# A two-layer mixture-of-experts kernel on one core: waits and small steps put in other places of four engines' orders, and the first layer's stores cut in two

## The chip, the core and the metric

The kernel runs on one core of a Trainium2 chip. Its time is the device time of one execution in microseconds (us). TensorE is called PE, VectorE DVE, ScalarE ACT, GpSimd POOL and SyncE SP; SP issues most of the transfers. PEld is PE's row of weight loads, and a small q behind an engine's name means its sequencer, which also does register loads.

## What is computed

The input x is 64 batches of 64 tokens by 1024 numbers. Each layer adds a correction to x:

```python
x = x + L0_ffn(L0_cond(x, id0))        # adapter: 64x64 matrix of the batch, over the tokens
x = x + L1_ffn(L1_cond(x, id1))        # adapter: 1024x1024 matrix of the batch
# L0_ffn: logits = y @ router_w.T + b; top 2 of 8 experts; h = y @ A_e (rank 16); out = sum gate*h @ B_e * 0.5
# L1_ffn: y @ base_w.T + b  +  0.5 * sum over the top 2 of 16 experts of gate * (y @ A) @ B_e (rank 64)
```

All of it is float32. The second layer's large products are made of three passes of split numbers (hi times hi, hi times lo, lo times hi), where `hi` is a rounded copy made by ACT and `lo` is the rest, made by DVE.

## The kernel before

Each engine has an order of its own, written out by hand; semaphores tie them together. There are three stages.

**First layer** (`two_groups(n)` on PE, n = 0 to 7, `NS` = 8). The batches go in 16 groups of four (`NG`), two to a round n. For a group PE makes z = x times router and A weights (`z_of`, L1573), mixes the tokens (`y_of`), DVE works out the gates of both groups of the next round (`gates0`, a chain of some 17 small operations from L1113 on, then four of L1117 that write `hw0`), PE turns `hw0` (`turn_h0`, L1619), and PE multiplies with the experts' B (`expand`, four quarters q). DVE adds x to each quarter (`add_x`, L1135) into one of two buffers `x1g`; `expand(g)` may write quarter q only when `add_x` has taken quarter q of group g-1. SP stores a group's `x1g` (1 MB, `store_x`, L457) when its four adds are done, then loads x for six groups later (`load_x`). `add_x(g, 0)` waits until the store of group g-2, from the same buffer, has landed. The first rounds of DVE's loop also hold constants for the second layer (`second_layer_constants`, L1066 to L1075) and register loads from `table`, the plan of the second layer (`w_used` L398, `start_of` L401, `alone` L406). PE does two of these loads after its last `expand`, behind eight filler products (`keep_going(8)`, L1626).

**Adapters of the second layer** (loops over u, the adapters in use, and j, the pairs of batches of an adapter; `step` on ACT and DVE, `y_of_pair` on PE). PE multiplies a pair with its adapter, turns the pair before it (`turn`, after chunk 1 of 8) and multiplies the turned pair with A and the router (`rh_of`, L1686, near the end). In the step at an adapter's last pair (`u_next` is given) ACT and DVE also split the next adapter's eight weight chunks (`w_chunks`, `low_chunks`, L830 and L1141), and `y_turned` (ACT L798, DVE L1217) splits the turned y between them. A pair with one batch (`lone`) takes PE two passes instead of three.

**Base product, routing and experts.** For 32 tiles t of 128 tokens PE runs `base_part(t, n)`, n = 0 to 15, three products each; ACT and DVE split the tile in quarters (`y_high` L877, `y_low` L1276). `expert_high` and `expert_low` (L896, L1286) split the 16 experts' B. DVE chooses the experts, gives each token its row, and makes one-hot tables `hot_a` (`tile_of_rows`) and `hot_b` (`row_of_rows(n)`, L1365, eight, two buffers). PE multiplies these (`row_sums(n)`, L1785, eight), which gives `rows`, the list by which POOL gathers tokens for the experts (L707); PE turns the gathered rows (`turn_hw`, L1795). After tile 7 the experts' products run between the base parts, then the rest of the tiles with the sum into the output.

## Time and profile before

| | |
|---|---|
| three runs, us | 1110.53, 1114.62, 1116.79 (median 1114.62) |
| profiled execution, us | 1110.44, its span 1108.8 |
| busy in the span, us | PE 1075.5, PEld 916.6, DVE 673.4, ACT 501.5, POOL 219.8 |
| granted clock of PE, mean | 0.995 of full |
| chain that ended last | PE 77%, DMA 7%, DVE 7%, ACT 3%, SPq 3%, issue 2% |

The span is the time from the first to the last record of the profiled execution. A busy PE holds waits between matmuls too short to show; what a change of order can give back is PE's idle time and what its clock loses after it. The chain names, from the end backwards, what each piece of work was released by.

### The profile page before, as it was taken

Reading aid. Unit: us, or ns where it says so; the run is one execution under the profiler, and the core shown is the slowest. Engines: PE = TensorE matmul, PEld = TensorE weight load, DVE = VectorE, ACT = ScalarE, POOL = GpSimd, SP = SyncE. Lnnn points to the kernel's source line nnn. Section 1 sums busy time; section 2 is a strip of 40 time slices with the busy share of each in tenths; the row PEclk is TensorE's granted clock in tenths of the full one; section 3 lists DMA queues with packets and bytes.
Section 4 is the critical chain, followed back from the end, with each engine's and each line's share of the span. In section 5 each row is a group of like instructions: output and inputs, shape, how many; then the busy total and the mean of one; then the engine's idle time right before and its main releaser. Section 6 shows DMA issues by size and latency. Waiting matters only on the chain.

```text
span 1108.8 us, 21632 instructions
## 1 busy us (share of the span) xinstructions
PE 1075.5 (97%) x5844; PEld 916.6 (83%) x5845; DVE 673.4 (61%) x1231; ACT 501.5 (45%) x1021; POOL 219.8 (20%) x354
## 2 busy tenths in 40 slices
PE   7989999999999999999999999999999999999998
PEld 7989878888887888888888877877777888888887
DVE  5778843755738457564546588545555466666666
ACT  1122123745638456564536642145555434443444
POOL 2211010110202011110101000155553322222220
PEclk9999999999999999999999999999999999999999
DMA  9678683673947648583677342279999999999996
GB/s 304 242 280 330 221 327 96 236 268 126 340 158 246 231 160 311 196 271 124 229 236 233 96 133 85 78 285 346 356 345 353 344 396 357 335 356 323 333 337 205
DMA packets 126125, 283.57 MB, mean 256 GB/s; under 512 B 28146, under 2 KB 35570, under 8 KB 124146
## 3 DMA queue, kind: packets, MB, share of 16 engines
q1 hardware_dynamic: 96592, 180.59, 46.1%
q0 software_dynamic: 29216, 102.25, 26.4%
q8 instruction: 29, 0.48, 0.2%
q14 instruction: 30, 0.25, 0.1%
q10 hardware_dynamic: 258, 0.01, 0.0%
HBM read 181.50 MB, written 101.29 MB: 255 GB/s over the span
## 4 chain that ended last, share of the span: by engine, by line
PE 77%; DMA 7%; DVE 7%; ACT 3%; SPq 3%; issue 2%; DVEq 0%; ACTq 0%
PE psum L1562 17%; PE psum L1564 16%; PE psum L1563 16%; PE psum L1686 4%; PE psum L1573 4%; DMA xp<-act_scratch 3%; PE psum L1809 3%; PE psum L1810 3%; PE psum L1678 3%; PE psum L1704 2%; PE psum L1706 2%; PE psum L1687 2%; PE psum L1818 1%; SPq L548 1%; ACT w L896 1%
## 5 line engine op out<-in xcount | busy, mean ns | idle before, releaser
L1562 PE MATMUL psum<-base_hi,xp_hi 128*128 128x512 f32 (+3 forms) x520 | 204.3, 393 | 4.4 <-DVE xp_lo L1276 4.2
L1563 PE MATMUL psum<-base_lo,xp_hi 128*128 128x512 f32 (+3 forms) x520 | 198.9, 383 | 0.0
L1564 PE MATMUL psum<-base_hi,xp_lo 128*128 128x512 f32 (+3 forms) x520 | 198.7, 382 | 0.0
L1562 PE MATMUL psum<-w,xp_hi 128*128 128x512 f32 x448 | 181.2, 404 | 0.0
L1564 PE MATMUL psum<-w,xp_lo 128*128 128x512 f32 x448 | 176.8, 395 | 0.0
L1563 PE MATMUL psum<-w,xp_hi 128*128 128x512 f32 x448 | 176.6, 394 | 0.0
L699 POOL DMA_DIRECT2D raw<-w1T x112 | 59.2, 528 | 414.8 <-DVE w L1141 393.4
L1141 DVE TENSOR_TENSOR w<-raw,w 128x1024 fp32r<-128x1024 f32 x112 | 132.2, 1220 | 11.5 <-ACT w L830 8.5
L877 ACT ACTIVATE xp_hi<-xp 128x256 fp32r<-128x256 f32 x124 | 51.2, 416 | 170.3 <-PE psum L1564 158.1
L1562 PEld LDWEIGHTS psum<-base_hi,xp_hi 128*128 128x128 f32 x520 | 98.1, 189 | 27.7 <-DVE xp_lo L1276 5.4
L1276 DVE TENSOR_TENSOR xp_lo<-xp,xp_hi 128x256 fp32r<-128x256 f32 x124 | 51.7, 424 | 108.5 <-ACT xp_hi L877 107.9
L1564 PEld LDWEIGHTS psum<-base_hi,xp_lo 128*128 128x128 f32 x520 | 98.1, 189 | 18.1
L1563 PEld LDWEIGHTS psum<-base_lo,xp_hi 128*128 128x128 f32 x520 | 98.2, 189 | 15.7
L707 POOL DMA_INDIRECT hwn<-rh_scratch,rows x80 | 75.8, 947 | 173.0 <-DVE rows L1375 112.1
L830 ACT ACTIVATE w<-raw 128x1024 fp32r<-128x1024 f32 x104 | 105.5, 1057 | 5.1 <-PE psum L1564 5.1
L1564 PEld LDWEIGHTS psum<-w,xp_lo 128*128 128x128 f32 x448 | 84.3, 188 | 19.6
L1562 PEld LDWEIGHTS psum<-w,xp_hi 128*128 128x128 f32 x448 | 84.5, 189 | 17.8 <-issue 1.2
L1563 PEld LDWEIGHTS psum<-w,xp_hi 128*128 128x128 f32 x448 | 84.6, 189 | 16.8
L943 ACT ACTIVATE x1t<-x1t,bias 128x128 f32<-128x128 f32 x256 | 78.1, 387 | 19.5 <-DMA x1t<-act_scratch 19.5
L1212 DVE COPY yp<-psum 128x512 f32 x28 | 19.4, 691 | 108.5 <-PE psum L1564 108.5
L790 ACT ACTIVATE yp<-psum 128x512 f32 x28 | 16.8, 599 | 135.6 <-PE psum L1564 135.6
L1198 DVE TENSOR_TENSOR xp_lo<-xp,xp_hi 128x512 fp32r<-128x512 f32 x58 | 39.9, 688 | 52.3 <-ACT xp_hi L780 52.3
(293 smaller groups left out, 1957.8 us busy)
## 6 DMA issues: line engine op xcount, KB each, us to landing
raw<-w1T POOLq DMA_DIRECT2D x120, 512.0 KB, 6.8
delta_scratch<-dl SPq DMA_DIRECT2D x80, 512.0 KB, 4.1
xp<-act_scratch SPq DMA_DIRECT2D x74, 256.0 KB, 3.3
act_scratch<-yT SPq DMA_DIRECT2D x72, 256.0 KB, 2.5
act_scratch<-x1g SPq DMA_DIRECT2D x16, 1024.0 KB, 5.2
x1t<-act_scratch SPq DMA_DIRECT2D x64, 256.0 KB, 4.8
out<-x1t SPq DMA_DIRECT2D x62, 256.0 KB, 5.4
xg<-xT SPq DMA_DIRECT2D x15, 1024.0 KB, 9.2
```

The source lines that it names most:

```text
L699: pool.dma_start(raw[:, i, :], w1T[bass.ds(a, 1), i, :, :].rearrange("a p k -> p (a k)")).then_inc(raw_in[i], 16)
L707: pool.indirect_dma_start(hwn[s % HRING][:, :], None, rhs[0:NB, :, :].rearrange("b c z -> (b c) z"), bass.IndirectOffsetOnAxis(ap=rows[:, ...
L830: act.activation(w_hi[:, i, :], raw[:, i, :], ACT.Copy).then_inc(w_hi_done, 1)
L877: act.activation(xp_hi[:, ks, :].rearrange("p i (b c) -> p b i c", b=2), xp[:, t % 2, :, ks, :], ACT.Copy).then_inc(yh_done, 1)
L943: last = act.activation(x[:, :, i, :], x[:, :, i, :], ACT.Identity, bias=bias[:, i:i + 1])
L1141: tt(w_lo[:, i, :], raw[:, i, :], w_hi[:, i, :].bitcast(F32), ALU.subtract).then_inc(w_lo_done, 1)
L1276: tt(xp_lo[:, ks, :].rearrange("p i (b c) -> p b i c", b=2), xp[:, t % 2, :, ks, :], xp_hi[:, ks, :].bitcast(F32).rearrange("p i (b c) -> ...
L1562: mm(out, a_hi, b_hi, start=start, stop=False, skip_group_check=True)
L1563: mm(out, a_hi, b_lo, start=False, stop=False, skip_group_check=True)
L1564: return mm(out, a_lo, b_hi, start=False, stop=stop, skip_group_check=True)
L1573: last = mm(z_ps[:, m, :], xg[slot][:, i, m * P:(m + 1) * P], p0[:, i, :], start=i == 0, stop=i == KC - 1)
L1686: mm(rh_ps, yq_hi[:, i, :], q2[:, i, :], start=i == 0, stop=False, skip_group_check=True)
```

## The change

Six edits, all of order but one:

1. `store_x` stores a group in two halves of 512 KB, each when its own two adds are done; in memory a half is 1 KB per partition and batch where the whole was 2 KB. The counts on `x1_out` are doubled to match.
2. `second_layer_constants` is cut in two. `sorting_constants` (six operations) stands in round 1 ahead of the adds of group 2, not behind them; `rank_constants` (two) in round 2 ahead of the adds of group 4. DVE's load of `used` follows these, and its loads of `total` and `one` stand in round 3 ahead of the adds of group 6; all three stood in round 2 behind the adds.
3. PE's loads of `used` and `total` stand in round 6 between the filler products and `turn_h0(7)`, not behind the last filler.
4. In a step with new weights, `y_turned` stands behind the first split chunk, not the second, on ACT and DVE.
5. On ACT, `expert_high(6)` and `(7)` stand inside the quarters of tile 2, not ahead of them.
6. `row_sums(n)` stand at n = 5, 7, ..., 15 of tile 6 and n = 1, 3 of tile 7, not at n = 1, 3, ..., 15 of tile 6.

```diff
             def store_x(g):
-                sp.wait_ge(x1_added, 4 * g + 4)
-                sp.dma_start(x1s[g * GB:(g + 1) * GB, :, :].rearrange("b p (i c) -> p b i c", c=C),
-                             x1g[g % 2][:, :, :, :]).then_inc(x1_out[g % 2], 16)
+                for h in range(2):
+                    ks = slice(h * KC // 2, (h + 1) * KC // 2)
+                    sp.wait_ge(x1_added, 4 * g + 2 * h + 2)
+                    sp.dma_start(x1s[g * GB:(g + 1) * GB, :, h * C * KC // 2:(h + 1) * C * KC // 2].rearrange(
+                        "b p (i c) -> p b i c", c=C), x1g[g % 2][:, :, ks, :]).then_inc(x1_out[g % 2], 16)
...
-                w_chunks(range(2))
+                w_chunks(range(1))
                 y_turned(j)
-                w_chunks(range(2, KC // 2))
+                w_chunks(range(1, KC // 2))
...
             keep(0)
-            expert_high(6)
-            expert_high(7)
             for t in range(2, FIRST + 1):
                 for q in range(4):
                     if t == FIRST and q == 3:
                         hw_high(0)
                     y_high(t, q)
+                    if t == 2 and q % 2 == 1:
+                        expert_high(6 + q // 2)
...
-            def second_layer_constants():
+            def sorting_constants():
...
+            def rank_constants():
+                dve.wait_ge(const_split_hi, 3)
                 for first, raw_part in ((0, q1raw), (R1 + E1, margin_raw)):
...
-                    dve.wait_ge(x1_out[g % 2], (g - g % 2) * 8 + 16)
+                    dve.wait_ge(x1_out[g % 2], (g - g % 2) * 16 + 16)
...
+                if n == 1:
+                    sorting_constants()
+                if n == 2:
+                    rank_constants()
+                    dve.wait_ge(table_ready, 1)
+                    used = w_used(dve)
+                if n == 3:
+                    total = start_of(dve, used)
+                    one = alone(dve, 0)
                 if n == NS - 2:
                     gates0(n + 1)
                 add_x(2 * n, 0)
                 add_x(2 * n, 1)
-                if n == 1:
-                    dve.wait_ge(const_split_hi, 3)
-                    second_layer_constants()
-                if n == 2:
-                    dve.wait_ge(table_ready, 1)
-                    used = w_used(dve)
-                    total = start_of(dve, used)
-                    one = alone(dve, 0)
...
                     keep_going(8)
+                    pe.wait_ge(table_ready, 1)
+                    used = w_used(pe)
+                    total = start_of(pe, used)
                     turn_h0(n + 1)
...
-                    if t == FIRST - 2 and n % 2 == 1:
-                        row_sums(n // 2)
+                    if t == FIRST - 2 and n % 2 == 1 and n > 3:
+                        row_sums((n - 5) // 2)
+                    if t == FIRST - 1 and n in (1, 3):
+                        row_sums(6 + n // 2)
```

DVE's order changes in the middle of rounds 1 and 2 of the first layer. Before, from the adds of group 2 (`x1g0<-psum,xg2`) to the gates of round 2 (the first row on `sm`):

```order
L1135 TENSOR_TENSOR x1g0<-psum,xg2 128x2x4x64 x4
L1066 TENSOR_SCALAR desc1<-idx 128x16
L1067 CAST iota<-idx 128x128
L1068 TENSOR_SCALAR tok<-idx 128x32
L1069 TENSOR_SCALAR tok<-tok 128x32
L1071 CAST ones<-raw 128x128
L1072 CAST before<-raw 128x128
L1075 TENSOR_TENSOR q2<-q1raw,q2 128x8x80
L1075 TENSOR_TENSOR q2<-margin_raw,q2 128x8x40
L1113 TENSOR_TENSOR sm<-psum,rbias 128x16 x2
```

The same place with the change (its line numbers are other ones):

```order
L1071 TENSOR_SCALAR tok<-tok 128x32
L1073 CAST ones<-raw 128x128
L1074 CAST before<-raw 128x128
L1140 TENSOR_TENSOR x1g0<-psum,xg2 128x2x4x64 x4
L1118 TENSOR_TENSOR sm<-psum,rbias 128x16 x2
```

Eight operations have left the place between the adds and the gates: six went ahead of the adds, and the two on `q2` a round later.

PE's order changes at the end of the first layer. Before, from the last filler products to the first matmul of the adapters:

```order
L1626 MATMUL psum<-b0_hi 128x512 x8
L398 TENSOR_LOAD table
L398 ISA x2
L401 ISA
L401 TENSOR_LOAD table
L401 ISA x2
L1717 UNCONDITIONAL_BRANCH
L1717 ISA
L427 TENSOR_LOAD table
L427 ISA x2
```

With the change:

```order
L1632 MATMUL psum<-b0_hi 128x512 x8
L1725 UNCONDITIONAL_BRANCH
L1725 ISA
L427 TENSOR_LOAD table
L427 ISA x2
```

Two register loads left this place; they stand behind the filler products of round 6, ahead of the four transposes of `hw0`.

ACT's order changes at the start of the base product. Before, from the copy of tile 0's sums (`nat0`) to that of tile 1's; `w<-raw` are the experts, `xp_hi<-xp` the quarters of tile 2:

```order
L887 ACTIVATE nat0<-psum 128x512
L887 ACTIVATE nat0<-psum 128x472
L896 ACTIVATE w<-raw 64x1024 x4
L877 ACTIVATE xp_hi<-xp 128x2x2x64 x4
L887 ACTIVATE nat1<-psum 128x512
L887 ACTIVATE nat1<-psum 128x472
```

With the change:

```order
L889 ACTIVATE nat0<-psum 128x512
L889 ACTIVATE nat0<-psum 128x472
L879 ACTIVATE xp_hi<-xp 128x2x2x64 x2
L898 ACTIVATE w<-raw 64x1024 x2
L879 ACTIVATE xp_hi<-xp 128x2x2x64 x2
L898 ACTIVATE w<-raw 64x1024 x2
```

The first two quarters of tile 2 moved ahead of all four expert operations, the last two ahead of two of them.

## Rows read from the trace of the kernel before

**Rows 1.** windows: busy us of PE, PEld, DVE, ACT, POOL; clock, DMA

```profile
0.00:145.00 145.00, 131.04 (x1065) 126.27 (x1067) 106.65 (x347) 25.65 (x55) 22.65 (x98) 1.00 0.76 276
```

**Rows 2.** waits of PE: in total, times, longest us

```profile
PE psum L1562 <- DVE xp_lo L1276: 4.2, 6, 1.4
...
PE psum L1562 <- DVE x1g L1135: 0.8, 1, 0.8
```

**Rows 3.** timeline, 50 to 75 us: start, duration, engine, line, idle before

```profile
50.50 0.17 DVE L1066 TENSOR_SCALAR desc<-idx 128x16 f32<-128x16 f32 x1
...
53.18 0.38 DVE L1113 TENSOR_TENSOR sm<-psum,rbias 128x16 f32<-128x16 f32 x2
...
58.12 0.66 PE L1619 MATMUL psum<-ident,hw 128*128 128x128 f32 x4 [1.69 <-DVE hw L1117]
...
63.77 0.69 DVE L1135 TENSOR_TENSOR x1g<-psum,xg 128x512 f32<-128x512 f32 x1 [2.31 <-PE psum L1564]
...
69.95 0.38 DVE L1113 TENSOR_TENSOR sm<-psum,rbias 128x16 f32<-128x16 f32 x2 [2.90 <-issue]
...
74.88 0.66 PE L1619 MATMUL psum<-ident,hw 128*128 128x128 f32 x4 [1.98 <-DVE hw L1117]
```

**Rows 4.** end of the first layer: chain, table loads, timelines of DVE and PE

```profile
135.81 4.24 DMA act_scratch<-x1g
...
L398 PEldq TENSOR_LOAD <-table x1: 502/502/502, 140.1 to 140.1; - x1
...
142.47 0.75 DVE L1193 TENSOR_TENSOR xp_hi<-xp,xp_hi 128x256 fp32r<-128x256 f32 x2
...
144.87 0.47 PE L1704 MATMUL psum<-w,xp_hi 128*128 128x512 f32 x1 [1.68 <-issue]
```

**Rows 5.** timeline and window around 356 us, two adapter changes in a row

```profile
356.15 0.38 PE L1686 MATMUL psum<-q,yq_hi 128*128 128x240 f32 x1 [2.19 <-DVE yq_lo L1217]
...
358.28 0.42 DVE L1193 TENSOR_TENSOR xp_hi<-xp,xp_hi 128x256 fp32r<-128x256 f32 x1
...
359.10 0.77 PE L1704 MATMUL psum<-w,xp_hi 128*128 128x512 f32 x1
...
360.00:362.00 2.00, 2.00 (x6) 1.52 (x5) 2.00 (x3) 2.00 (x3) 0.92 (x2) 0.50 0.95 304
```

**Rows 6.** timelines of ACT and DVE at the first tiles of the base product

```profile
639.91 4.31 ACT L896 ACTIVATE w<-raw 64x1024 fp32r<-64x1024 f32 x4
...
640.08 2.47 DVE L1286 TENSOR_TENSOR w<-raw,w 64x1024 fp32r<-64x1024 f32 x2
```

**Rows 7.** timelines and window, 685 to 725 us: the row sums and after

```profile
687.70 0.42 ACT L877 ACTIVATE xp_hi<-xp 128x256 fp32r<-128x256 f32 x1 [2.26 <-PE psum L1564]
...
690.37 0.42 ACT L877 ACTIVATE xp_hi<-xp 128x256 fp32r<-128x256 f32 x1 [2.25 <-PE psum L1564]
...
693.00 2.35 DVE L1365 TENSOR_TENSOR hot_b<-iota,place_f 128x1024 fp32r<-128x1024 f32 x2
...
694.37 1.31 PE L1785 MATMUL psum<-hot_a,hot_b 128*128 128x80 f32 x8 [2.69 <-DVE hot_b L1365]
...
696.00:698.00 2.00, 2.00 (x6) 1.63 (x5) 0.00 (x0) 0.00 (x0) 0.00 (x0) 0.50 0.05 17
...
698.08 1.15 PE L1785 MATMUL psum<-hot_a,hot_b 128*128 128x80 f32 x8
...
700.47 1.06 PE L1785 MATMUL psum<-hot_a,hot_b 128*128 128x80 f32 x8
...
713.98 1.02 POOL L707 DMA_INDIRECT hwn<-rh_scratch,rows  x1 [112.13 <-DVE rows L1375]
...
722.33 0.38 PE L1795 MATMUL psum<-ident,hwn 128*128 128x128 f32 x2
```

**Rows 8.** DMA issues, 650 to 720 us: queue, count, KB each, us to landing

```profile
base_scratch<-nat SPq DMA_DIRECT2D x5, 492.0 KB, 2.9
...
margin<-side_scratch SPq DMA_DIRECT2D x1, 640.0 KB, 6.6
```

More of the change, by code:

```diff
@@ L473, in _ @@
                 for s in range(2):
-                    sp.wait_ge(x1_out[s], (b // (2 * GB)) * 16 + 32)
+                    sp.wait_ge(x1_out[s], (b // (2 * GB)) * 32 + 48)
                 sp.dma_start(xp[:, bass.ds(slot_of(1, total), 1), h, :, :].rearrange("p a i c -> p (a i) c"),
@@ L477, in _ @@
             for s in range(2):
-                sp.wait_ge(x1_out[s], 16 + 16 * (NG // 2))
+                sp.wait_ge(x1_out[s], 16 + 32 * (NG // 2))
             def load_pair(j):
@@ L689, in _ @@
                 for s in range(2):
-                    pool.wait_ge(x1_out[s], (b // (2 * GB)) * 16 + 32)
+                    pool.wait_ge(x1_out[s], (b // (2 * GB)) * 32 + 48)
                 pool.dma_start(xp[:, bass.ds(slot_of(0, total), 1), h, :, :].rearrange("p a i c -> p (a i) c"),
@@ L693, in _ @@
             for s in range(2):
-                pool.wait_ge(x1_out[s], 16 + 16 * (NG // 2))
+                pool.wait_ge(x1_out[s], 16 + 32 * (NG // 2))
             with pool.Fori(1, used + 1) as u:
@@ L856, in _ @@
             for s in range(2):
-                act.wait_ge(x1_out[s], 16 + 16 * (NG // 2))
+                act.wait_ge(x1_out[s], 16 + 32 * (NG // 2))
             with act.Fori(0, used) as u:
@@ L1240, in low_chunks @@
                             w_low(u_next, i)
-                low_chunks(range(2))
+                low_chunks(range(1))
                 y_turned(j, 0)
@@ L1245, in step @@
                 y_turned(j, 1)
-                low_chunks(range(2, KC // 2))
+                low_chunks(range(1, KC // 2))
                 x_low(j + 1, 0, one)
@@ L1260, in _ @@
             for s in range(2):
-                dve.wait_ge(x1_out[s], 16 + 16 * (NG // 2))
+                dve.wait_ge(x1_out[s], 16 + 32 * (NG // 2))
             with dve.Fori(0, used) as u:
@@ L1644, in two_groups @@
                     z_of(2 * n + 4, 1)
+                return (used, total) if n == NS - 2 else None
             pe.wait_ge(ident_done, 2)
@@ L1665, in _ @@
             for n in range(NS):
-                two_groups(n)
+                counts = two_groups(n)
+                if n == NS - 2:
+                    used, total = counts
             keep_going(8)
-            pe.wait_ge(table_ready, 1)
             def turn(v):
@@ L1714, in _ @@
             pe.wait_ge(const_split, 3)
-            used = w_used(pe)
-            total = start_of(pe, used)
             with pe.Fori(0, used) as u:
```

## The prediction

> **What bounds the kernel now.** I read the table of windows first, to see how much of PE's time is idle, then PE's chain of waits, to see who ends the idle time, and then the timeline at each place that the change touches. PE is the bound: 1075.5 of the 1108.8 us of the span are busy, so the edits can give back at most some 33 us. The first layer holds 14 of them in its 145 us, start-up included, and its DMA share is 0.76, so the transfers have gaps there [rows 1]. In the whole table of PE's waits only a few entries are long, and each lies where an edit works. I take them in order of time. Times of before are quoted throughout, and all of it is one profiled execution.
>
> **The rounds' gates (edit 2).** At 58.12 PE begins to turn `hw0` of round 2 after 1.69 us of idleness, at 74.88 that of round 3 after 1.98 us; both times the gates on DVE are late [rows 3]. What makes them late stands ahead of them on DVE: from 50.50 to 53.18, 2.68 us of constants, and in the next round 2.90 us in which DVE sits idle by "issue" before 69.95, which are its register loads [rows 3]. Both exceed PE's wait, so with them gone PE's data come first and the waits go: 1.69 + 1.98 = 3.67 us. The moved work lands where DVE waits for PE: 2.31 us idle before 63.77 [rows 3]. The two `q2` operations read 960 columns, where the add of 512 took 0.69 us, so 1.3 us, and one load of three is a third of the 2.90, 1.0 us: together they just fill that gap. In round 1 the six others, the 1.4 us that are left of the 2.68, need such a gap too. In round 3 the two other loads (1.9 us) go ahead of the adds of group 6, where DVE is idle less; the adds may start a microsecond late, but the next `expand` asks for them one quarter at a time and over 2 us later. Behind them stand the gates of round 4, which can be late by a few tenths. I take 3.6 us, with 2.5 and 3.7 as ends.
>
> **The end of the first layer (edits 1 and 3).** PE is idle 1.68 us before its first adapter product at 144.87 [rows 4], so its fillers ended at 143.19. Its data are complete at 143.22, when DVE ends the split of pair 0 [rows 4]. The rest is PE's sequencer: it begins the first of three table loads at 140.1 [rows 4] and comes to the product 4.8 us later, 1.6 us a load with what stands between. Without two of them it could be there at 141.7, so that the fillers' end and the split bound it, both 143.2: a gain of 1.65 us. Where the two loads go, in round 6, PE waits for the gates behind its fillers anyway, and the sequencer runs ahead, as 140.1 against fillers that end at 143.19 shows; without that cover they would cost their 3.2 us there.
>
> The cut stores move these two bounds too. A store of 1 MB took 4.24 us to land and released DVE's adds of group 15 [rows 4]; the one before it delayed those of group 14, and through them PE, 0.8 us [rows 2]. A transfer of 492 KB lands in 2.9 us [rows 8]. So the second half lands about 1.3 us sooner after the same add, PE loses its 0.8 us of waiting, its fillers end at 142.4, and the split of pair 0 ends near 141.9. Together the adapters start about 2.5 us sooner. If halves land no sooner it is 1.65; if the sequencer needs its 1.68 us for other things than the loads, only the 0.8.
>
> The price of the cut is in the packets: 512 more of 1 KB per group, 32 on each of 16 DMA engines. No row has a 1 KB packet, so I bound it. Below it is nothing: the bytes are the same. Above: 640 KB in 4096 packets of 160 bytes landed in 6.6 us [rows 8]. The two stores, 1 MB in 4.24 us and 492 KB in 2.9, give 2.6 us for moving 1 MB and 1.6 for the rest. Less that rest it is 5.0 us for 256 packets an engine, 20 ns each with their bytes. 32 of them are 0.6 us a group, against gaps that are 24% of the stage [rows 1]. I take nothing, as the gaps hide it; SP's second issue, 0.4 us a group, is hidden as well, SP being idle between groups.
>
> A rule speaks against this edit. The Trainium skill, "DMA: Bandwidth & Descriptors", section "Measured", says to batch transfers to at least 1 MiB, and its section "Anatomy of one DMA" gives an estimate of 2.0 us plus bytes by 436 GB/s: 4.4 us for the whole store, 3.2 us for a half, two halves 6.4 us if one came after the other. The rows, 4.24 and 2.9 us, agree with the two single figures. By the rule the stores would cost 2 us more a group; but only the last half is waited for, so the sum by its figures would be 1.2 us sooner where rows give 1.3.
>
> **The step with new weights (edit 4).** PE waits for the split of turned y once, 2.19 us at 356.15 [rows 5], where two adapters change in a row and DVE is busy all the time, 2.00 of 2 us [rows 5]. One chunk (1.2 us) fewer stands ahead of it now. But the same chunk then stands ahead of the split of the next pair, which ends where it did, at 358.70 [rows 5], and PE's next product began at 359.10 [rows 5]. DVE's work is the same in sum, so what the edit gives at one wait it takes at the next: 0.4 us. PE's clock fell to 0.50 here [rows 5], for some 7 us; even at 1.00 PE would wait for DVE's copy of y a little later, so at most 0.8 us come back. Lower end: nothing.
>
> **The experts' split on ACT (edit 5).** At 639.91 ACT does four expert operations in 4.31 us before the quarters of tile 2 [rows 6], and PE's longest wait for a low quarter is 1.4 us, at 645.3 [rows 2]. With the first two quarters ahead, these are done at 640.8; then DVE is the limit, busy with experts until 642.55 [rows 6], so its two quarters end at 643.3, before PE's need at 643.9. The wait goes: 1.4 us. The four operations themselves are needed by DVE only 12 us later.
>
> **The row sums (edit 6).** PE wants `hot_b` after two parts of tile 6 and waits 2.69 us, to 694.37 [rows 7]; DVE's first two are 1.2 us each from 693.00 on [rows 7]. Four parts take 2.67 us (687.70 to 690.37 [rows 7]). Asked for four parts later, PE comes at 694.35 by its own work: the wait goes, with nothing to spare. After that wait the clock was 0.50 [rows 7], and the step from the first sums to the second took 3.71 us against 2.39 for the next one [rows 7]: 1.3 us, and 0.2 more in the sums. So 2.69 + 1.5 = 4.2 us; if the wait shrinks only by half and the clock still falls, 1.3.
>
> What is late next: the last sums end about 711.5, 1.6 us sooner than before, while PE is 4.2 us sooner. POOL's first gather then starts at 712.4 instead of 713.98 [rows 7], the second 1.5 us later, and gathers land in 2.6 us, so at 716.5. PE wants them at 722.33 - 4.2 = 718.1 [rows 7]. That leaves 1.6 us. The later gathers stay ahead by more.
>
> **The sum.** 3.6 + 2.5 + 0.4 + 1.4 + 4.2 = 12.1 us. Against the profiled execution's own 1110.44 that is 1098.3; against the median of the three runs, 1114.62, it is 1102.5. I predict 1100.5, between these. The lower ends add to 2.5 + 0.8 + 0 + 1.4 + 1.3 = 6.0, the upper to 3.7 + 2.6 + 0.8 + 1.4 + 4.3 = 12.8. What a measurement of this kernel can tell from no change is about 0.5%, 5.6 us.
>
> **The rivals.**
> - *The row sums or the gathers are still waited for* (0.18). The margin is 0.02 us for `hot_b` and 1.6 for the gathers. For it: DVE's place between its fixed chain and PE is exact only in this execution. Against it: both engines start that stretch from the same tile. It costs about 3 us of the 12.1: 1103.5.
> - *The first layer gives nothing* (0.10). Loads of x are issued behind the stores, and a PE that runs 3.6 us ahead could find them late. For it: most of the stage's idle DMA time lies in a few gaps. Against it: stores, and so loads, move ahead with PE. Then 12.1 - 6.1 = 6.0 remain: 1106.5.
> - *A new half-clock stretch* (0.06). Waits of about 2 us in other places could make the clock fall as at 356.15; each costs the wait and up to 3.5 us at half speed [rows 5]. Two leave about 1.5 us: 1111.
> - *More than I forecast* (0.07): the clock no longer falls at 356, and the runs above 1110 lose what set them apart. 1095.
> - *Slower: packets of 1 KB at half rate* (0.03). If each extra packet cost as much as a whole one of 2 KB, 80 ns by the 2.6 us of moving for 32 packets an engine, the 16 stores would add 41 us to the 0.76 of 145 [rows 1], 151 us in all. With some 12 us at the stage's start and end that no transfer can fill (an estimate) it would last 163 us, 18 more, and with the 6.0 us of the other edits the whole would end near 1122. It decides against the change, by over 0.5%, from about 67 ns a packet on; the bound above is 20.
>
> The forecast itself has 0.56. **How the numbers follow.** 1100.5 is the likeliest case. The range 1094 to 1108 holds the forecast's 1096 to 1104, the rival with the row sums, the one without the first layer and most of the faster one; outside are the half-clock case, the slower one and the tails, under 0.2. Faster by over 0.5% (below 1109): the forecast, the first two rivals and the faster one, less what scatter of the runs takes, 0.87. Within: 0.10. Slower: 0.03.
>
> **What would show it.** PE's waits at L1619 for `hw` near 58 and 73 us gone; the first adapter product near 138.7 (144.87 - 3.6 - 2.5); the wait for y's split shrunk to about 1 us and followed by one for the split of the pair; no wait for the low quarter of tile 2; row sums entered with under 0.3 us of waiting and a clock of 1.00; the first gather about 10 us sooner. I would be wrong if stores of 512 KB took 4 us or more to land, if loads of x held up L1573, or if a clock of 0.50 appeared at a place where it was not.

## The result, and the profile after

The changed kernel took 1101.84 us in the median of four runs (1100.9 to 1102.03), the kernel before 1112.57 beside it (also four, 1110.49 to 1116.79), and 1100.5 was predicted, 1.34 us less. The measurement gives a ratio of 0.9888 with a 95% interval of 0.985 to 0.9926. Its ratios, here and below, are not quotients of the two medians: that would be 0.9904 here, and elsewhere the two differ by up to 0.0014. Its profiled execution took 1100.9 us with a span of 1099.3, 9.5 us less than the span of before.

The sum had worked with 12.1 us, and the two profiles differ by 9.5, so I laid the two traces beside each other at events that both have. First PE's waits in the changed kernel (us in total, times, longest us), the rows that answer to [rows 2]:

```profile
PE psum L1826 <- DVE fin L1482: 3.4, 4, 1.9
PE psum L1714 <- DVE xp_hi L1199: 2.1, 1, 2.1
...
PE psum L1568 <- DVE xp_lo L1204: 1.9, 1, 1.9
PE psum L1568 <- DVE xp_lo L1282: 1.6, 3, 0.6
PE psum L1625 <- DVE hw L1122: 1.2, 2, 1.0
...
PE psum L1696 <- DVE yq_lo L1223: 1.0, 1, 1.0
```

The waits for the low quarters fell from 4.2 us to 1.6, those for the adds and for `hot_b` are gone. New is the second kind of `xp_lo`, 1.9 us at L1204: the split of a pair of batches in the adapters' stage, for which PE did not wait before. The same places in the windows and timelines, as [rows 1], [rows 3], [rows 4], [rows 5] and [rows 7] show them of before (a timeline row is the start, the duration, the engine and line, what it does, and in brackets the idle time ahead of it and what ended that; a row of a window ends in the granted clock, the DMA share and GB/s, and the clock has two levels in these rows, 1.00 and 0.50):

```profile
0.00:145.00 145.00, 138.16 (x1096) 132.38 (x1098) 107.65 (x349) 26.74 (x57) 24.74 (x102) 1.00 0.81 283
...
55.72 0.49 PE L1625 MATMUL psum<-ident,hw 128*128 128x128 f32 x3
...
70.66 0.60 PE L1625 MATMUL psum<-ident,hw 128*128 128x128 f32 x4
...
137.69 0.75 DVE L1199 TENSOR_TENSOR xp_hi<-xp,xp_hi 128x256 fp32r<-128x256 f32 x2
...
138.55 0.47 PE L1714 MATMUL psum<-w,xp_hi 128*128 128x512 f32 x1
...
352.37 0.38 PE L1696 MATMUL psum<-q,yq_hi 128*128 128x240 f32 x1 [1.04 <-DVE yq_lo L1223]
...
356.45 0.77 PE L1714 MATMUL psum<-w,xp_hi 128*128 128x512 f32 x1 [2.07 <-DVE xp_hi L1199]
...
690.74 1.06 PE L1793 MATMUL psum<-hot_a,hot_b 128*128 128x80 f32 x8
693.05 0.98 PE L1793 MATMUL psum<-hot_a,hot_b 128*128 128x80 f32 x8
...
696.00:698.00 2.00, 2.00 (x15) 1.79 (x14) 1.93 (x4) 0.28 (x1) 0.00 (x0) 1.00 0.00 0
...
708.32 1.28 POOL L709 DMA_INDIRECT hwn<-rh_scratch,rows  x1 [108.17 <-DVE rows L1381]
...
714.01 0.38 PE L1803 MATMUL psum<-ident,hwn 128*128 128x128 f32 x2
```

The turns of rounds 2 and 3 have no bracket: no wait. The first adapter product stands at 138.55, where 138.7 was predicted, 6.3 us sooner than before. The row sums enter without a wait at full clock. But `turn_hw` is 8.3 us sooner, not 12. What lies between is shown by the chain of waits (start, duration, what), the timelines of POOL and PE, and a window:

```profile
137.80 3.42 DMA act_scratch<-x1g
141.52 0.46 issue
142.07 0.39 SPq L477
...
143.47 5.17 DMA xp<-act_scratch
148.83 0.64 ACT xp_hi L782
149.67 0.70 DVE xp_lo L1204
```

```profile
142.74 0.53 POOL L701 DMA_DIRECT2D raw<-w1T  x1 [19.04 <-issue]
...
150.77 0.69 PE L1568 MATMUL psum<-w,xp_hi 128*128 128x512 f32 x1 [1.92 <-DVE xp_lo L1204]
...
152.00:154.00 2.00, 2.00 (x6) 1.52 (x6) 2.00 (x6) 0.82 (x3) 0.00 (x0) 0.50 1.02 414
```

The last half store is issued at 137.80 and lands 3.42 us later. SP loads x of pair 1, the adapters' second pair, in two transfers, the first issued at 142.07, the second at 143.47. POOL waits for that landing and begins at 142.74 with eight loads of the next adapter's weights, 4 MB. The second transfer of x takes 5.17 us beside them, PE waits 1.92 us and then runs at a clock of 0.50. In the kernel before POOL's first load stood at 148.43, behind both transfers (146.65 and 148.04), and the second landed in 3.4 us, 0.2 us ahead of ACT's need.

To follow this through all kernels I use distances between events that each has, so that the start, which varies, drops out. "Round 0" is the start of PE's first turn of `hw0`; then come the time from it to the turn of round 7, from there to the first adapter turn, to the second adapter turn, to ACT's first copy of `nat`, to DVE's first `hot_b`, to PE's first `turn_hw`, and to ACT's last `y_high`. They are differences of starts in the timelines of one profile each.

| kernel | round 0 | to round 7 | to 1st turn | to 2nd turn | to `nat` | to `hot_b` | to `turn_hw` | to last `y_high` |
|---|---|---|---|---|---|---|---|---|
| before | 26.73 | 103.99 | 16.09 | 11.03 | 481.00 | 54.16 | 29.33 | 367.33 |
| changed | 26.19 | 100.62 | 13.69 | 14.69 | 481.94 | 52.25 | 24.63 | 366.13 |
| e1 edit 2 only | 30.33 | 100.64 | 16.12 | 11.05 | 481.46 | 54.16 | 29.32 | 367.69 |
| e2 edit 1 only | 26.53 | 106.40 | 16.87 | 11.36 | 480.18 | 54.17 | 33.70 | 368.14 |
| e3 edit 3 only | 28.99 | 105.64 | 14.53 | 11.05 | 481.92 | 54.16 | 29.29 | 365.48 |
| e4 changed, less edit 4 | 27.08 | 100.65 | 13.66 | 14.45 | 481.62 | 52.24 | 24.63 | 367.98 |
| e5 changed, weights behind | 26.50 | 100.65 | 13.67 | 11.04 | 480.91 | 52.23 | 24.64 | 367.69 |
| e6 changed, look-ups first | 26.25 | 100.64 | 13.66 | 17.11 | 480.73 | 52.24 | 24.63 | 368.87 |
| e7 changed, less edit 1 | 27.86 | 100.63 | 14.53 | 11.03 | 480.80 | 52.24 | 24.63 | 370.44 |
| e8 edits 5 and 6 only | 26.34 | 105.59 | 16.09 | 11.03 | 481.35 | 52.23 | 24.65 | 369.60 |
| e9 changed, again | 28.74 | 100.65 | 13.65 | 15.97 | 480.67 | 52.24 | 24.64 | 371.02 |
| e10 as e5, less edit 4 | 28.79 | 100.63 | 13.64 | 11.03 | 481.61 | 52.23 | 24.64 | 376.98 |
| e11 changed, sums two parts later | 25.83 | 100.64 | 13.65 | 16.10 | 481.86 | 52.24 | 25.96 | 370.41 |
| e12 changed, halves by batch | 25.98 | 100.64 | 14.33 | 11.92 | 480.72 | 52.23 | 24.64 | 374.79 |

From before to changed: -0.54 - 3.37 - 2.40 + 3.66 + 0.94 - 1.91 - 4.70 - 1.20 = -9.52 us, the difference of the spans. Several columns repeat to 0.03 us in kernel after kernel; the first, the fifth and the last do not, in kernels that don't differ there. A single pair of profiles says nothing finer than some 2 us on those.

Part of the start's scatter can be read. In e1, e3, e9 and e10 the clock is at 0.50 for a while behind a wait of 2.0 to 2.3 us for x near 15 us, and these four are the late ones, with 28.7 to 30.3 us to round 0; in the other ten it stays at 1.00 from 13 us on, and they need 25.8 to 27.9 (e4 and e7 among them, with waits of 2.1 and 2.4 us). e1 and before at the same place:

```profile
18.00:20.00 2.00, 2.00 (x13) 1.71 (x13) 0.48 (x3) 0.00 (x0) 0.00 (x0) 0.50 1.00 412
18.00:20.00 2.00, 2.00 (x19) 2.00 (x19) 1.68 (x10) 0.00 (x0) 0.37 (x2) 1.00 1.05 430
```

### The profile page after: what moved, and what is told of

The parts are those of the page before. It is cut to its first block, busy times and chain, and to the rows that moved or that the text cites. A ratio compares the mean times of both kernels' runs of the same rounds, so it can differ in the third digit from the quotient of the medians.

```text
span 1099.3 us, 21647 instructions
## 1 busy us (share of the span) xinstructions
PE 1076.2 (98%) x5844; PEld 916.7 (83%) x5845; DVE 672.9 (61%) x1231; ACT 500.6 (46%) x1021; POOL 222.5 (20%) x354
## 4 chain that ended last, share of the span: by engine, by line
PE 82%; DMA 7%; DVE 3%; SPq 3%; issue 2%; ACT 2%; ACTq 0%; DVEq 0%
PE psum L1568 19%; PE psum L1570 18%; PE psum L1569 18%; PE psum L1579 5%; PE psum L1696 4%; DMA xp<-act_scratch 4%; PE psum L1818 3%; PE psum L1817 3%; PE psum L1688 3%; PE psum L1714 2%; PE psum L1716 2%; PE psum L1697 1%; PE psum L1826 1%; SPq L550 1%; DMA out<-x1t 1%
## 5 line engine op out<-in xcount | busy, mean ns | idle before, releaser
L1568 PEld LDWEIGHTS psum<-base_hi,xp_hi 128*128 128x128 f32 x520 | 97.8, 188 | 26.7 <-issue 6.1
L1204 DVE TENSOR_TENSOR xp_lo<-xp,xp_hi 128x512 fp32r<-128x512 f32 x58 | 39.9, 688 | 56.4 <-ACT xp_hi L782 56.4
```

Source lines behind the costliest of these rows:

```text
L1568: mm(out, a_hi, b_hi, start=start, stop=False, skip_group_check=True)
```

## The experiments

**e1, edit 2 alone.** The diff is DVE's part of the change in the first layer, on the kernel before.

> The kernel before with edit 2 alone (constants and DVE's table loads ahead of the adds). Theory A (PE's own work sets the time and the first layer keeps what it gains): PE's waits of 1.69 and 1.98 us ahead of the turns of rounds 2 and 3 are gone, the first adapter product comes 3.7 us sooner apart from the start-up's scatter, and nothing is given back, because DVE, the stores and pair 1's load move with PE: from the first to the second turn of an adapter pair 11.0 us as before, span about 3.7 us shorter, 0.33%. Theory B (what edit 2 gives is what is lost at pair 1): that distance grows to about 14.7 us and the span hardly changes.

Measured: median 1111.17 us (ten runs) against 1114.48 of the kernel before (25 runs), ratio 0.9971, interval 0.9949 to 0.9992. Rounds 0 to 7 take 100.64 us, 3.35 less than in the profile of before, and pair 1 is reached as before, 11.05. Theory A holds, with 0.3 us less: the two waits of 3.67 us are gone, but round 3 itself takes 14.95 where it took 14.62. The span, 1110.1, shows none of it because this execution reached round 0 3.6 us later (30.33 against 26.73), the one with the longest stretch of 0.50 at the start.

**e2, edit 1 alone.** The diff is `store_x` and its counts.

> The kernel before with edit 1 alone (stores of 512 KB). Theory A: the second half lands 3.4 us after its issue instead of 4.24 for a whole store, PE loses its wait of 0.8 us for the adds of group 14, and still waits for its register loads ahead of the first adapter product, so the end of the first layer comes 0.8 us sooner; span 0.8 us shorter, within what can be measured of no change. Packets cost nothing: rounds 14.9 us apart as before. Rival (packets of 1 KB slow the loads of x): a wait of PE for x in the first layer's z products, and a span longer than before by 1 us or more.

Measured: median 1117.18 (ten runs), ratio 1.0024, interval 1.0004 to 1.0043: slightly slower. The second half lands in 3.39 us, and DVE's split of pair 0 starts 10.90 us after the turn of round 7 (143.83 - 132.93) where it started 11.75 after it (142.47 - 130.72 [rows 4]): the 0.85 us are there. No wait for x at L1575 but the one at the start, 1.5 us, which before has too. What it loses stands elsewhere: DVE's load of `used` took 1.94 us instead of 0.56, so PE waited 2.8 us at round 3 and ran at 0.50 behind it (in [rows 3] it waited 1.98 and did not); and the half-speed stretch behind the row sums lasted from 696 to 710, where before it was over within the window 698:700:

```profile
696.00:698.00 2.00, 1.12 (x6) 1.16 (x6) 1.86 (x2) 0.00 (x0) 0.00 (x0) 0.64 0.74 201
708.00:710.00 2.00, 2.00 (x8) 1.71 (x7) 0.00 (x0) 0.25 (x1) 0.00 (x0) 0.50 0.00 0
```

(Both windows are of e2; the clock is the third number from the end.) That alone is 4.4 us, 33.70 against 29.33 in the table. Edit 6 has no part in e2, so a kernel with the row sums in their old place can meet this; how often, no trace here shows, and neither is it shown that e2's ten runs were slower for it.

The order of the loads is in e2 already as in the changed kernel: POOL's first load goes out at 148.87, SP's second transfer of x at 149.6, and it takes 6.3 us. But there it costs next to nothing, since the register loads still hold PE back:

```profile
146.60 0.47 PE L1706 MATMUL psum<-w,xp_hi 128*128 128x512 f32 x1 [2.08 <-issue]
...
156.10 0.63 ACT L782 ACTIVATE xp_hi<-xp 128x512 fp32r x1 [4.17 <-DMA xp<-act_scratch]
```

ACT waits 4.17 us for x, PE hardly, and the second turn comes 11.36 us behind the first, 0.3 more than before.

**e3, edit 3 alone.**

```diff
                     keep_going(8)
+                    pe.wait_ge(table_ready, 1)
+                    used = w_used(pe)
+                    total = start_of(pe, used)
                     turn_h0(n + 1)
```

> The kernel before with edit 3 alone (PE's two register loads moved to round 6). Theory A: the 1.68 us of idleness ahead of the first adapter product go to about 0.2, so that it comes 1.5 us sooner. Pair 1's second half of x landed at 151.4 before, 0.2 us ahead of ACT's need at 151.61; it does not move with PE, so ACT waits for it 1.3 us. PE had about 1.4 us of slack there, so its own wait is between 0 and 0.3 us, the clock stays at 1.00, and the distance between the first two turns is 11.0 to 11.4. Rival (the clock falls as soon as x is later than PE): distance 12 us or more and the span no shorter than before.

Measured: median 1112.46 (ten runs), ratio 0.9991, interval 0.9957 to 1.0026. The first turn comes 1.56 us sooner behind round 7 and the second 11.05 behind the first: theory A. Its first layer shows what edit 2 can be worth in another execution. PE waits 2.01 us at round 3, as before with its 1.98, but now the clock falls:

```profile
77.13 0.52 PE L1619 MATMUL psum<-ident,hw 128*128 128x128 f32 x2 [2.01 <-DVE hw L1117]
...
78.00:79.00 1.00, 1.00 (x6) 1.00 (x5) 1.00 (x2) 0.66 (x2) 0.00 (x0) 0.50 0.57 234
```

and rounds 0 to 7 take 105.64 us, 1.65 more than before and 5.0 more than with edit 2. e8, which has neither, shows the same 105.59.

**e4, the changed kernel without edit 4.** `w_chunks` and `low_chunks` take `range(2)` and `range(2, KC // 2)` again.

> The changed kernel with edit 4 undone (two split chunks ahead of the turned y in a step with new weights). Theory A (edit 4 gives nothing and costs 0.55 us by a longer stretch at half clock): PE waits 2.2 us at the split of the turned y and under 0.5 at the split of the lone pair, and from the turn at 344.7 to the one at 372.2, 27.5 us after the change, it takes 26.95 as in the kernel before. Theory B (the 0.55 us came from the place in time, not from the edit): it takes 27.5 or more here too. Either way the whole differs from the changed kernel by under 1 us in the median.

Measured: median 1103.76 (four runs), 0.9899, interval 0.9859 to 0.9939. The waits come back as 2.2 and 1.0 us, and over the double change (turn to turn across both pairs) PE takes 27.55 us, with edit 4 27.51. Theory B: the half microsecond lost there was not edit 4's. Over all profiles that distance is 26.3 to 27.6 in the seven kernels with edit 4 and 26.2 to 27.6 in the seven without, means 26.7 and 27.2: the 0.4 us predicted can be in it, but isn't shown. What sorts the distances is how long the clock stays at 0.50 behind PE's wait there: some 3 us in six kernels (e2, e5, e6, e7, e9, e12), 26.2 to 26.6, and some 7 us in the other eight, 27.0 to 27.6, two of them with edit 4. In the changed kernel and in e5, both windows some 4 us behind the same wait:

```profile
360.00:362.00 2.00, 2.00 (x10) 2.00 (x9) 2.00 (x2) 0.65 (x2) 0.38 (x1) 0.50 1.04 417
357.00:359.00 2.00, 2.00 (x13) 1.73 (x12) 2.00 (x4) 1.09 (x2) 0.53 (x1) 1.00 1.05 423
```

Among kernels with the same stretch, edit 4 gives nothing that shows. Whether it makes the short one likelier (five of seven with it, one of seven without) these few profiles don't settle.

**e5, the weights' loads behind pair 1's x.**

```diff
+            pool.wait_ge(xp_in, 32)
             with pool.Fori(1, used + 1) as u:
```

> The changed kernel with POOL's eight loads of the next adapter's weights (4 MB) held back until pair 1's x has landed. Theory A (pair 1's x is late because its second half shares the DMA engines with these loads, 5.17 us against 3.4 in the kernel before): it lands about 3.2 us after its issue, ACT waits 3 us instead of 4.92, PE's 1.92 us of waiting shrink to 0 to 0.3, the clock stays at 1.00, and from the first to the second turn it takes 11.0 to 11.4 us instead of 14.7: 3.3 to 3.7 us off the changed kernel, ratio about 0.988 x 0.997 = 0.985. Theory B (the landing of the last stores and SP's look-ups set it, not the sharing): the transfer still takes over 4.5 us, the distance stays above 14, no gain. Third case: the adapter's weights become late in their turn, a wait for raw near 190 us or for the second adapter.

Measured: median 1100.57 (six runs, the kernel before 1114.58 beside it), ratio 0.9876, interval 0.985 to 0.9902. The second transfer of x, issued at 143.8, lands in 2.9 us, and POOL loads from 148.34 on. ACT waits 2.70 us, PE not at all, and the second turn is 11.04 us behind the first:

```profile
146.97 0.63 ACT L783 ACTIVATE xp_hi<-xp 128x512 fp32r x1 [2.70 <-DMA xp<-act_scratch]
...
148.34 0.54 POOL L702 DMA_DIRECT2D raw<-w1T  x1 [24.31 <-issue]
```

(Timelines of e5.) Theory A: in the trace the whole 3.65 us come back, and PE waits for no adapter's weights later. The ratio is not as low as the 0.985 expected, and the runs alone, 0.9876 against 0.9888 of the changed kernel, don't show the gain.

**e6, both look-ups ahead of the wait.**

```diff
+            pair_1 = [sp.value_load(table[0:1, T_LOAD + 2 + h:T_LOAD + 3 + h], ...) for h in range(2)]
-            for h in range(2):
-                b = sp.value_load(table[0:1, T_LOAD + 2 + h:T_LOAD + 3 + h], min_val=0, max_val=NB - 1)
+            for h, b in enumerate(pair_1):
```

> The changed kernel with both of SP's look-ups for pair 1 ahead of the wait for the last stores. The second half of x is issued 0.4 us behind the first instead of 1.4, so 1.0 us sooner. Theory A: it lands 1.0 to 1.8 us sooner (less of it shares with the weights' loads), PE's wait falls from 1.9 to between 0.1 and 0.9, too short for the clock to fall as the other waits of about 1 us show, and the first two turns are 11.2 to 12 us apart: 2.7 to 3.5 us off the changed kernel. Theory B (sharing alone decides, and the transfer just takes as much longer): wait 1.5 or more and the clock falls again, gain under 1 us.

Measured: 1103.35 (six runs), 0.9888, interval 0.986 to 0.9916, nothing gained that shows. Both theories had the issue wrong: the first transfer was issued 0.6 us later than in the changed kernel (142.71) and the second no sooner (143.5), since SP did both look-ups first and its waits afterwards. POOL's first load stood 0.7 us ahead of the second transfer as in the changed kernel (142.86), and this one took 6.74 us:

```profile
143.54 6.74 DMA xp<-act_scratch
```

(chain of waits of e6.) PE waited 3.5 us and the turns lay 17.11 apart. The longer transfer isn't this edit's doing: in the six kernels in which POOL's first load is issued 0.7 us ahead of the second transfer of x, this lands in 5.17 (changed), 6.3 (e2), 4.9 (e4), 6.74 (e6), 6.4 (e9) and 6.5 us (e11), and in the eight where POOL comes behind it, in 2.8 to 3.4 (2.8 in e7 and e10, 3.4 in before and e1).

**e7, the changed kernel with whole stores.**

> The changed kernel with edit 1 undone (stores of 1 MB again). Theory A (the halves bring 0.85 us at the end of the first layer and nothing else): PE waits 0.8 us for the adds of group 14, from the turn of round 7 to the first adapter turn it takes 14.5 us instead of 13.7, pair 1's x is issued 0.9 us later, and it is late against PE by the same as with halves, so that the second turn comes 14.4 to 14.7 us after the first and the clock falls: 0.8 us slower than the changed kernel. DVE's register load of the number of adapters, 1.00 and 1.21 us in the two kernels with halves and 0.56 in those without (1.94 in the kernel before with halves alone), takes 0.56 again if the halves slow it, and about 1 if its place does.

Measured: 1100.19 (four runs, 1096.28 to 1102.93), 0.9857, interval 0.9822 to 0.9892. To the first turn it takes 14.53 us, 0.84 more than with halves, as expected. But the second turn then follows after 11.03: PE doesn't wait, where I had expected 14.4 to 14.7. I had expected that SP and POOL both follow the landing. The issues show that they don't (timelines of e7):

```profile
140.41 0.37 SPq L457 DMA_DIRECT2D act_scratch<-x1g  x1
144.41 1.77 SPq L475 DMA_DIRECT2D xp<-act_scratch  x2
...
146.19 0.54 POOL L699 DMA_DIRECT2D raw<-w1T  x1 [20.47 <-issue]
```

SP's second transfer of x goes out 5.4 us after its last store (145.8), POOL's first load 5.8 after. With halves it is 5.7 (143.47 - 137.80) and 4.9 (142.74 - 137.80). SP is held by its own four register loads, which begin after the last store is issued; in e7 its first transfer (144.41) goes out before the last store has landed (144.66). POOL is held by the landing, which came 0.8 us sooner with halves. So the quicker landing released the wrong load first. Beside edit 3, edit 1 gave 0.84 us and took 3.66; without edit 3 it took 0.3 (e2).

**e8, edits 5 and 6 alone**, on the kernel before.

> The kernel before with edits 5 and 6 alone. Theory A: 1.9 us at tile 2 and 4.7 at the row sums or more, as the other two kernels with these edits show against the profile of before, nothing given back, so its span is 6.6 us shorter than that of a kernel before with the same start-up, ratio 0.993 to 0.994. Since PE's half-speed stretch behind the row sums lasted 3 us in one kernel without edit 6 and 13 us in another, the gain on the median can exceed it: then 0.991 to 0.993. Rival (gathers or expert products late in their turn): a gain of 4 us or less, with PE waits behind 720 us that the kernel before does not have.

Measured: 1107.67 (five runs), 0.9925, interval 0.9894 to 0.9955. 1.93 and 4.68 us in the two columns, together 6.6, as in all kernels with these edits, and no new kind of wait behind `turn_hw`. The last column is 2.3 us longer than that of before, in it PE's waits for `fin` 4.9 us rather than 3.9, and behind one of them, of 1.94 us at 893.6, the clock is at 0.50 for some 3 us. The same is seen in e7 (2.51 us at 889.0), and in none of the first ten profiles besides. Over the first ten profiles of the table it is 365.5 to 368.1 in the four without edit 6 and 366.1 to 370.4 in the six with it, 1.3 us more in the mean. Those two have the longest last stages of the ten (370.4 and 369.6), so part of the difference is that; whether edit 6 gives something back there, nothing here settles.

**e9, the changed kernel again, and e10, e5 without edit 4**, side by side on another chip.

> The changed kernel once more, beside its improved version on the same chip. All theories: the pattern of its first profile comes back, since it does not hang on chance: 100.6 us from the turn of round 0 to that of round 7, 13.7 to the first adapter turn, 14.4 to 14.7 to the second with the clock at 0.50 in between, 83.2 us from the third quarter of tile 1 to the end of the row sums' stretch. What may differ is the start (26 to 30 us to the first turn) and the expert stage (367 to 372 us in the profiles so far), so a span of 1098 to 1105 and a median of 1100 to 1103.

> The changed kernel with the weights' loads behind pair 1's x, and edit 4 undone. Theory A (edit 4 is worth nothing, the order of the loads 3.5 us): 11.0 us from the first to the second adapter turn, 26.2 to 27.6 us over the double change of adapter as in every kernel so far, with one wait of 2.2 us at the turned y and one of 1.0 at the lone pair in place of 1.0 and 2.1; median 3.5 us below that of the changed kernel run beside it, 1097 to 1100. Theory B (edit 4 gives 0.4 us or more): over the double change 0.4 us longer than with edit 4.

Measured: e9 1108.65 (twelve runs), e10 1105.72 (six), the kernel before 1117.38 (23): 0.9919, interval 0.9894 to 0.9944, and 0.9887, interval 0.985 to 0.9925. e10 loses nothing at pair 1 (11.03), e9 more than the first profile: PE waits 3.2 us and the turns are 15.97 apart, where I had allowed 14.7; its median and span lie above my ranges too, on a chip on which the kernel before also takes longer. The difference of the medians, 2.9 us, is in the direction of the 3.5 expected, but the intervals overlap. The last column was outside my range as well in e10. All four kernels run on this chip, e9 to e12, take longer behind the row sums: from the first `turn_hw` to the third 10.8 us in e9 (716.56 to 727.31), 6.7 in the changed kernel (714.01 to 720.68), with the clock down to 0.50 in between:

```profile
726.00:728.00 2.00, 2.00 (x7) 1.58 (x6) 0.00 (x0) 0.00 (x0) 0.00 (x0) 0.50 0.69 248
```

(a window of e9). PE's longest waits for `dl`, the copies of the experts' products, are 1.2 to 3.0 us there, but records of PE, ACT and DVE are missing, so the trace doesn't say who was late, and no kernel without edit 6 has a profile from this chip. Whether edit 6 takes part in it is open.

**e11, the row sums two parts later, not four.**

```diff
-                    if t == FIRST - 2 and n % 2 == 1 and n > 3:
-                        row_sums((n - 5) // 2)
-                    if t == FIRST - 1 and n in (1, 3):
-                        row_sums(6 + n // 2)
+                    if t == FIRST - 2 and n % 2 == 1 and n > 1:
+                        row_sums((n - 3) // 2)
+                    if t == FIRST - 1 and n == 1:
+                        row_sums(7)
```

> The changed kernel with the row sums two base parts later than in the kernel before, not four. PE then asks for the first one-hot table 1.33 us sooner than now, when DVE ends it at the same time: it waits 1.3 us. Theory A (edit 6 is a wait of 2.69 and a clock that only a long wait costs): the clock stays at 1.00, and the stretch is 1.3 us longer than in the changed kernel, of the 4.7 us 3.4 remain. Rival (any wait there starts a half-speed stretch): 0.50 behind the wait and 3 us or more lost.

Measured: 1110.87 (ten runs, beside e9's 1108.65), 0.9944, interval 0.9917 to 0.9971. The wait and the clock of the whole stretch:

```profile
691.68 1.06 PE L1793 MATMUL psum<-hot_a,hot_b 128*128 128x80 f32 x8 [1.34 <-DVE hot_b L1371]
...
688.00:700.00 12.00, 10.65 (x64) 9.28 (x63) 11.04 (x14) 1.88 (x5) 0.00 (x0) 1.00 0.25 87
```

1.34 us of wait and 1.32 us longer to `turn_hw` (25.96 against 24.64): the wait costs itself and no more. So of the 4.7 us of edit 6 some 2.7 are wait and the other 2.0 went with the clock of 0.50. The medians differ by 2.2 us, with intervals that overlap.

**e12, halves by batch.** Two transfers of 512 KB with 2 KB packets, both issued after the fourth add; one run, 1106.92.

```diff
+                sp.wait_ge(x1_added, 4 * g + 4)
                 for h in range(2):
-                    ks = slice(h * KC // 2, (h + 1) * KC // 2)
-                    sp.wait_ge(x1_added, 4 * g + 2 * h + 2)
+                    bs = slice(h * GB // 2, (h + 1) * GB // 2)
...
```

> The changed kernel with each group's store cut by batches and not by chunks: two transfers of 512 KB with packets of 2 KB, both issued when all four adds are done. Theory A (packets of 1 KB and the time of the issue are two things): the last of the two is issued 0.4 us later than a whole store would be and lands in 3.4 us or more after its issue, about 0.4 us sooner than the whole; PE waits some 0.4 us for the adds of group 14. DVE's load of the number of adapters took 1.0 to 1.4 us in four kernels with packets of 1 KB and 0.56 in those with 2 KB: 0.56 if the packets slow it, 1.0 or more if the second transfer does. Pair 1: the loads of weights begin before or with the second half of x, so the turns are 13 to 14.7 us apart.

Measured: DVE's load of `used` takes 0.56 us again, against 1.00 to 1.94 in the eight kernels with halves by chunk and 0.56 in those with whole stores. So not the second transfer slows it; packets of 1 KB do, or the earlier issue that goes with them, which e12 undid as well. PE waits 0.8 us for the adds, so the landing isn't sooner for DVE, and the second turn comes after 11.92 us: POOL's first load (145.87) stood behind the second transfer of x (144.9) here, not ahead as I had expected, because the last half, issued 0.4 us behind the other, took longer to land than a whole store does (4.25 in e7):

```profile
138.75 5.57 DMA act_scratch<-x1g
```

(chain of waits of e12.)

## Why the prediction was right, and where not

The time was right, and four of the six edits gave what their steps said to within half a microsecond (2, 3, 5 and 6); edit 4's share isn't shown, and edit 1 gave its term and took back more than that. The last was missed, and that the total still came within 1.34 us is in part luck, as the sum at the end shows.

- **Edit 2**, 3.6 forecast, 3.35 measured. The waits went as worked out, the few tenths lost in round 3 were named. The three register loads were not a third of the 2.90 us each, though: before they took DVE 0.56, 0.34 and 1.49 us, in e1 0.56, 0.33 and 0.31. Against executions in which the clock falls behind that wait it is 5.0 (e3, e8).
- **Edits 1 and 3**, 2.5 forecast, 2.4 to the first adapter turn, of it 1.56 by the loads (e3; forecast 1.65) and 0.84 by the halves (e7; forecast 0.85). The packets cost nothing that shows in the rounds, 14.94 us each with halves and without; the slower rival had nothing behind it. A stated sign of being wrong, halves that take 4 us or more to land, did appear: from 28 to 125 us, beside the loads of x, a half took 5.2 us in the median, where a whole store took 5.5. It did no harm, since PE waited for none of these; the last halves landed in 3.4. The Trainium skill, "DMA: Bandwidth & Descriptors", section "Anatomy of one DMA", gives an estimate of 3.2 us for 512 KB, fitted to transfers that POOL issues, while these are SP's: the trace's 3.4 is close to it for the last halves, 5.2 is not. That page's advice in "Measured", to batch to 1 MiB, would have been right here by the traces (e7), though not for the reason it gives, the share of the peak bandwidth.
- **The step that failed** is "The cut stores move these two bounds too". It asked who on PE's path waits for a landing and stopped there. It didn't ask what else the landing releases. Counted from the last store, POOL's 4 MB of weights were let off 0.8 us sooner while SP's load of pair 1, held by SP's register loads, was not, and x landed late: 1.92 us of waiting and 1.7 of half clock, 3.66 in all. e5 (order restored) and e7 (landing late again) both remove it. It takes edits 1 and 3 together: from the first turn to the second it is 11.05 us with edit 3 alone (e3), 11.36 with edit 1 alone, though x took 6.3 us to land (e2), and 14.45 to 17.11 in the five profiles that have both and the order of the changed kernel. So the step also failed to ask what PE, 2.4 us sooner, needs next: before, x was there 0.2 us ahead of ACT. It is the rival "a new half-clock stretch", which had 0.06 and no place, and one of the signs of being wrong that the prediction names, a clock of 0.50 where it was not.
- **Edit 4**, 0.4 forecast. The wait shrank to 1.04 and the next grew to 2.07, 3.1 us in sum, where before had one wait of 2.2 and the other kernels without the edit 2.2 and another 0.6 to 1.0. No gain is shown: the distance over the change went by the length of the half-speed stretch (e4).
- **Edit 5**, 1.4 forecast, 1.9 measured in all ten kernels with it. The term was read from the longest wait alone; the whole stretch gave half a microsecond more.
- **Edit 6**, 4.2 forecast, 4.7 measured: 2.7 of wait, as said, and 2.0 of clock for the 1.5 taken from two steps. The margin of 0.02 us at `hot_b` held in every kernel that has edit 6 as it stands, and the gathers landed in time in the first profile. The last stage was 1.3 us longer in the mean with this edit, not resolved. The first gather was 5.7 us sooner than before and not 10, since PE reached that stage with less.
- **The sum.** 3.35 + 2.4 + 1.9 + 4.7 = 12.4 us, less 3.7 at pair 1, is 8.7, where 12.1 was forecast. (In the other profiles with this order pair 1 lost 3.4 to 6.1, so 8.7 is near the upper end of what the change gives.) The rest of the 9.5 is chance: 0.5 at the start and 1.2 at the end, less 0.9 in the adapters. The runs beside it had 1112.57 as the median of before, and 1112.57 less 8.7 is 1103.9. The measured 1101.84 is 2 us better, which four runs can't tell from it. So the sum was 3.4 us too large, and scatter of the runs made good some 2 us of it: that part of the hit is luck.

e5's version, with the weights behind x, had a ratio of 0.9876, and 0.9887 as e10, where e9 beside it had 0.9919; e7, with whole stores, had the lowest of all, 0.9857. Against the changed kernel neither is outside the intervals; in the traces both have the second turn 3.65 us sooner behind the first.

## What to carry to other kernels

When a transfer lands sooner, list everything that its semaphore releases on every queue, and in which order these go out: a large prefetch that gets ahead of a small, urgent load costs more than the landing gave. Make such an order explicit with a wait, as e5 does, instead of leaving it to which engine happens to be held longer. And compare profiles by distances between events: here the start and the last stage moved by up to 4.5 and 11.5 us on their own, while a change of 0.3 us in between repeated to some hundredths.

## What the hardware showed that was not expected

- The length of a wait did not decide alone whether the clock fell. It went to 0.50 behind waits of PE of 1.69 (e4, pair 1), 1.92 (changed kernel, pair 1), 1.96 (e8, round 3) and 2.01 us (e3, round 3), and stayed at 1.00 after 1.68 (before, first adapter product), 1.98 (before, round 3) and 2.37 us (e2, at 905.70). The stretch at half speed behind `hot_b`'s 2.7 us lasted 3 us in one execution and 13 in another. The rows of e4 and of e2, each with its window:

```profile
151.42 0.64 PE L1568 MATMUL psum<-w,xp_hi 128*128 128x512 f32 x1 [1.69 <-DVE xp_lo L1204]
152.00:154.00 2.00, 2.00 (x7) 1.51 (x6) 2.00 (x4) 1.53 (x4) 0.00 (x0) 0.50 1.01 410
...
905.70 0.44 PE L1820 MATMUL psum<-ident,fin 128*128 128x128 f32 x2 [2.37 <-DVE fin L1478]
905.00:907.00 2.00, 1.30 (x10) 1.25 (x11) 2.00 (x4) 0.19 (x1) 0.94 (x1) 1.00 1.05 421
```

- DVE's load of `used` from `table` took 0.56 us in the six kernels with 2 KB packets and 1.0 to 1.9 in the eight with 1 KB packets. Packets aren't all that such a load depends on: the third load (L406) took 1.49 us in before, e3 and e8, all with 2 KB packets, and 0.31 in e1, where it stands a round later.
- A transfer of 256 KB landed in 2.8 to 3.4 us when it was issued ahead of POOL's run of 512 KB transfers, by as little as 0.4 us (e7), and in 4.9 to 6.7 us when it was issued 0.7 us behind the first of them.
